# The section ahead of head 0 in 16 slots in place of 20, with projections and maxima moved to earlier slots

## What is computed

```python
qkv = einsum('bte,fe->btf', x, Wqkv); q, k, v = split(...)      # 8 heads, D = 64
q = q + pe;  k = k + pe                                         # positions
scores = where(causal, einsum('bhtd,bhsd->bhts', q, k) / sqrt(D), -inf)
probs = softmax(scores);  attn = einsum('bhts,bhsd->bhtd', probs, v)
x = layernorm(x + einsum('btf,ef->bte', attn, Wo))
x = layernorm(x + ffn(x))                                       # not touched
```

## Time and profile before

| | us |
|---|---|
| Median of 3 runs (732.24 to 735.25) | 733.39 |
| The profiled execution's own time | 734.77 |
| Its span in the trace | 733.0 |
| TensorE busy | 654.5 |
| VectorE / GpSimd / ScalarE busy | 504.9 / 503.1 / 449.2 |
| First score pair of head 0 starts at | 48.29 |

### The profile page before, as it was taken

How to read it: one execution, slowest core, us unless ns; L and a number is a source line. 1 busy time by engine, 2 the same in 40 slices (tenths; PEclk the granted TensorE clock), 3 DMA queues, 4 the chain that set the end, 5 groups by cost and what they waited for, 6 DMA issues and landing times. The chain is left out here.

```text
span 733.0 us, 10119 instructions
## 1 busy us (share of the span) xinstructions
PE 654.5 (89%) x3215; PEld 497.5 (68%) x3215; DVE 504.9 (69%) x1048; ACT 449.2 (61%) x626; POOL 503.1 (69%) x289
## 2 busy tenths in 40 slices
PE   5789999999999999999999999999877899989873
PEld 4557777777777777777677777777667687666651
DVE  3577667667766766866776676674187978877684
ACT  3436666676666666667667666667636577756551
POOL 6016887887878788788787778879943456667560
PEclk9979999999999999999999999999988899999995
DMA  7423211222112221122211232103300000000000
GB/s 186 110 64 70 61 44 45 46 69 60 44 43 49 69 58 44 44 51 69 55 44 44 53 71 51 45 1 91 98 2 1 0 1 1 0 16 0 14 1 29
DMA packets 27460, 33.75 MB, mean 46 GB/s; under 512 B 6897, under 2 KB 13842, under 8 KB 27282
## 3 DMA queue, kind: packets, MB, share of 16 engines
q1 hardware_dynamic: 27410, 33.14, 19.0%
HBM read 6.84 MB, written 1.05 MB: 11 GB/s over the span
## 5 line engine op out<-in xcount | busy, mean ns | idle before, releaser
L313 POOL TENSOR_TENSOR probs_l<-probs,probs_h 128x1024 fp32r<-128x1024 f32 (+1 forms) x160 | 347.5, 2177 | 132.0 <-PE o_ps L536 73.6
L407 DVE TENSOR_REDUCE m_part<-max_ps 128x1 f32<-128x512 f32 (+2 forms) x320 | 181.0, 605 | 111.0 <-PE max_ps L483 79.6
L350 ACT ACTIVATE probs<-scores 128x1024 f32<-128x1024 f32 (+1 forms) x160 | 150.3, 940 | 153.9 <-PE scores L511 96.7
L536 PE MATMUL o_ps<-probs_h,v 128*128 128x512 f32 (+5 forms) x640 | 185.2, 373 | 24.6 <-DVE oh L386 24.1
L353 ACT ACTIVATE probs_h<-scores 128x1024 fp32r<-128x1024 f32 (+1 forms) x160 | 149.8, 936 | 0.0
L536 PEld LDWEIGHTS o_ps<-probs_h,v 128*128 128x128 f32 (+1 forms) x640 | 95.9, 162 | 48.3 <-issue 20.0
L814 POOL TENSOR_TENSOR hid_lo<-hid,hid_hi 128x512 fp32r<-128x512 f32 x64 | 86.6, 1359 | 55.0 <-ACT hid_hi L894 42.3
L510 PE MATMUL scores<-q,k 128*128 128x512 f32 (+1 forms) x320 | 122.8, 384 | 0.0
L511 PE MATMUL scores<-q,k 128*128 128x512 f32 (+1 forms) x320 | 116.9, 365 | 0.0
L536 PE MATMUL o_ps<-probs_l,v 128*128 128x512 f32 (+1 forms) x320 | 116.4, 364 | 0.0
L483 PE MATMUL max_ps<-k,q 128*128 128x512 f32 (+2 forms) x320 | 103.1, 398 | 7.4 <-DVE m_part L407 6.2
(11 more groups left out here) (195 smaller groups left out, 986.9 us busy)
## 6 DMA issues: line engine op xcount, KB each, us to landing
k<-qk SPq DMA_DIRECT2D x96, 128.0 KB, 2.3
q<-qk SPq DMA_DIRECT2D x96, 128.0 KB, 2.3
q<-m_turn SPq DMA_DIRECT2D x128, 0.5 KB
v_all<-L_ffn_ew SPq DMA_DIRECT2D x2, 768.0 KB, 6.5
pos<-positions SPq DMA_DIRECT2D x1, 1024.0 KB, 6.8
out<-v_all SPq DMA_DIRECT2D x4, 256.0 KB, 2.3
acc<-L_attn_Wqkv SPq DMA_DIRECT2D x2, 256.0 KB, 3.9
v_all<-L_attn_Wo SPq DMA_DIRECT2D x2, 256.0 KB, 6.4
```

The costliest lines, as they stand in the source:

```text
L313: pool.tensor_tensor(probs_l[:, p % 2, :, lo:CH], probs[:, p % 2, :, lo:CH], probs_h[:, n % 3, :, lo:CH], ALU.subtract).then_inc(S["probs_ ...
L350: act.activation(probs[:, p % 2, :, lo:CH], scores[:, p % 2, :, lo:CH], ACT.Exp, scale=D ** -0.5).then_inc(S["probs_ready"], 1)
L407: dve.tensor_reduce(m_part[:, r, j:j + 1], max_ps[:, u % 2, 0:width], AX.X, ALU.max).then_inc(S["tile_max_ready"], 1)
L536: last = pe.matmul(o_ps[0:rows, lo:CH], v, pr, start=(p == PAIR0[c] and j == 0 and k == 0), stop=(p == PAIR0[c + 1] - 1 and j == 1 and k = ...
```

## The change

`section(-1)` has NT = 16 slots in place of 20. In it the projections stand at slots 0, 2, 5 and 9 (before 0, 6, 10, 16), each followed by its copies in the slot after (1, 3, 6, 10), and the first 22 pieces of maxima of head 0, two a slot, go from slot 5 to 15 (before 9 to 19). Both are now beside the tiles of v, which stay one a slot in slots 0 to 15. The low half of head 0's v moves from slots 16 and 18 of that section to slots 0 and 1 of `section(0)`. TensorE waits for the copies of all tiles of v ahead of `section(0)`, since the four banks are the scores' from there on. All other sections are as they were.

```diff
+V_HIGH, V_LOW, FIRST_V_LOW = 15, (16, 18), (0, 1)
+FIRST_PROJECT = {0: 0, 2: 1, 5: 2, 9: 3}
+FIRST_UNITS = 5
 def due(table, p, after, h):
+    if h < 0:
+        return [(FIRST_PROJECT[p - after], 0)] if table is PROJECT and p - after in FIRST_PROJECT else []
 def units(p, h):
+    if h < 0:
+        for n in (2 * (p - FIRST_UNITS), 2 * (p - FIRST_UNITS) + 1):
+            if n >= 0:
+                yield 0, n
+        return
             def section(h):
-                for p in range(NP):
+                for p in range(NP if h >= 0 else NT):
@@ VectorE
+            def v_low(h, part):
+                b, ts = h % 2, slice(part * NT // 2, (part + 1) * NT // 2)
+                dve.wait_ge(S["v_high_ready"], h + 1)
+                dve.tensor_tensor(v2[:, b, ts, :], v_all[:, h, ts, :], v1[:, b, ts, 0:D], ALU.subtract).then_inc(S["v_low_ready"], 1)
-                    if p in V_LOW and 0 <= h + 1 < H:
+                    if p in V_LOW and 0 < h + 1 < H:
+                        v_low(h + 1, V_LOW.index(p))
+                    if p in FIRST_V_LOW and h == 0:
+                        v_low(h, FIRST_V_LOW.index(p))
@@ TensorE
             section(-1)
             pe.wait_ge(S["ones_beside_v_made"], 2)
             pe.wait_ge(S["rows_beside_qk_made"], 3)
+            pe.wait_ge(S["v_copied"], NT)
             for h in range(H + 1):
                 section(h)
```

More of the change, by code:

```diff
@@ L115 @@
 OUTPUT = {5: (3, -1), 7: (0, 0), 12: (1, 0), 19: (2, 0)}
-V_HIGH, V_LOW = 15, (16, 18)
+V_HIGH, V_LOW, FIRST_V_LOW = 15, (16, 18), (0, 1)
 DONE = {PAIR0[c + 1] + 2: (c, 0) for c in range(NC)}
+FIRST_PROJECT = {0: 0, 2: 1, 5: 2, 9: 3}
+FIRST_UNITS = 5
 def due(table, p, after, h):
+    if h < 0:
+        return [(FIRST_PROJECT[p - after], 0)] if table is PROJECT and p - after in FIRST_PROJECT else []
     for slot, (c, ahead) in table.items():
```

## The result

| | before | changed |
|---|---|---|
| median of 5 runs, us | 733.13 (732.24 to 735.25) | 740.99 (739.27 to 741.34) |
| profiled execution, us | 734.77 | 741.34 |
| its span, us | 733.0 | 739.5 |

The ratio is 1.0100 with a 95% interval of 1.0077 to 1.0124: 7.9 us slower, where 736.0 and a range of 732.5 to 739.0 were forecast.

What follows compares the result with a forecast made beforehand. The prediction took TensorE, in fixed order, to bound the heads, so only head 0's start could move: +3.55 - 2.15 + 1.25 = +2.65 us on 733.39 gave 736.0 us, range 732.5 to 739.0.

Steps and rivals of the forecast that it cites:

- the two long waits: Ahead of head 0: TensorE idle from about 18.7 to 21.5 us and from 30.4 to 34.4 us.
- the main point: Slot 6: VectorE reduces pieces 2 and 3 only after chunk 2's low part, at 33.77 us; TensorE idles until 34.4.
- First term: Slots ahead of head 0: first score pair at 51.85 us against 48.29, +3.55 us.
- Second term: Head 0's slot 0: first to second score pair takes 2.2 us at the higher clock, before 4.35; -2.15 us.
- Third term: Head 0's low half of v: two pieces, 0.68 us each, delay the first product with v; +1.25 us.
- The second rival: Lower clock persists in slots 11 to 15 or head 0's slot 0: 738.2 to 739.6 us, chance 0.20.
- other place: Sign of failure: the clock at 1.2 GHz in another place than 34 to 39 us.
- The rival that was to be faster: Pieces 2 and 3 reduced near 30.4 us, before the wait for chunk 2: 730.9 or 729.0 us, chance 0.07.
- The prediction's paragraph on ordering: VectorE's queue ahead of head 0: strict FIFO, so waiting reductions cannot pass chunk 2's low part and the sum stands.
- the third rival: Old stalls ahead of head 0 worth as much as new ones: -0.9 to +1.2 us, 732.5 to 734.6, chance 0.23.
- the fourth: Changed kernel faster, with pieces 2 and 3 reduced ahead of chunk 2's wait: 730.9 or 729.0 us, chance 0.07.

Runs made afterwards that it cites:

- e3: Changed kernel with chunk 2's projection at slot 6 in place of 5: 739.40 us, ratio 1.0081.
- e5: The changed kernel run and traced a second time, nothing altered: 740.56 us, ratio 1.0092.
- e2: Changed kernel with both low pieces of head 0's v first in head 0's slot 0: 737.71 us, ratio 1.0059.
- e1: Kernel before with only head 0's two low pieces of v moved, to slots 0 and 1 of head 0: 735.35 us, ratio 1.0028.
- e12: Kernel before with head 0's two low pieces of v moved to the very start of head 0's slot 0: 733.40 us, ratio 0.9997.
- e6: e2 with 15 matmuls that nobody reads added ahead of piece 4: 737.05 us, ratio 1.0048.
- e8: Changed kernel with low v pieces first in head 0, chunk 2 at slot 6, and a later wait for v's last two copies: 736.15 us, ratio 1.0043.
- e10: e8 with unread matmuls in two waits, 11 ahead of chunk 1's projection and 7 ahead of piece 6: 737.05 us, ratio 1.0049.
- e11: Kernel before with chunk 3's projection at slot 13 in place of 16 and unread matmuls ahead of pieces 6 and 12: 734.27 us, ratio 1.0008.
- e7: Kernel before with unread matmuls in two waits, 8 ahead of piece 6 and 9 ahead of piece 18: 730.97 us, ratio 0.9965.
- e9: Kernel before with only the 9 unread matmuls ahead of piece 18: 732.13 us, ratio 0.9989.

## Why the prediction was wrong

**Right.** The prediction was right that TensorE's queue is the kernel's and that a late head 0 shifts the whole: from product 2 (6.31 us late) to the end of the heads (6.23 late) nothing is won back. It was right that chunks 0 to 2 don't move, and on the two long waits: 2.62 and 3.64 us stand where the steps had 2.85 and 4.0. That VectorE's order behind chunk 2's low part is the main point is not borne out: e3 undid it, and the first pair came only 0.5 to 0.9 us earlier.

**First term, +3.55 for the first score pair: 4.33 measured (3.87 in e5).** Nearly all of the difference is chunk 3's high part, 22.12 after the start point where 21.47 was reckoned: its positions were added 0.4 us late (39.98 against 20.52 from the start point), and ScalarE's copy of tile 9, at 40.67, stood ahead of it. From piece 12 (24.18) to the first pair (32.44) took 8.26 us where the steps have 8.25.

**Second term, -2.15 for the clock in head 0's slot 0: -1.92.** 53.91 - 51.48 = 2.43 against 4.35.

**Third term, +1.25 for the low half of v: this is the step that failed.** It took "0.68 each" from the earlier trace rows, a row of a time in which GpSimd does nothing, and used it at a time when GpSimd works. The piece took 2.49. From the second score pair to product 1 the change cost 6.42 - 3.81 = 2.61 us, twice the term; in e2, where no piece is held, it cost 5.13 - 3.81 = 1.32. e1 gives the same move alone, 1.80 us at the first product and 1.9 us of time; e12 gives it without the overlap, 0.

**A low clock in no term.** From product 1 to product 2 took 3.98 us, 2.69 before: another 1.29, at 1.2 GHz. It would be easy to charge this to the held piece too, since TensorE's wait of 2.86 us behind that piece comes just ahead. The runs don't bear that out. In e1 the piece is held and TensorE waits 1.91 us, and no low clock follows; in e2 nothing is held, TensorE waits 1.79 us, and it does. In e6, where the wait of 3.65 us ahead of head 0 is filled, a wait of 1.81 us at the same place is not followed by it. So what TensorE did earlier seems to count as well, and which wait made this stretch stays open. The second rival had a low clock in head 0, but in its first slot and for 2.15 us; by the prediction's own signs, 60 to 63 us is the "other place" that was not to be.

Sum by the trace: 4.33 - 1.92 + 2.61 + 1.29 = 6.31 at product 2, against 2.65. The third term is 1.36 of the 3.66 us between them, the low clock 1.29, the first term 0.78, the second 0.23. With the end of the heads 6.23 late, the start point 1.14 earlier and the rest 1.5 longer this is the 6.5 between the two spans.

**The base.** The medians differ by 7.9, in e5's session by 6.9; the profiled executions by 6.57. The profiled execution of before was 1.6 above its median, that of the changed kernel 0.35. This 0.3 to 1.3 us is in no term. The places of the low clock in setup and rest move single executions by more than that, but that they make this difference is not shown.

**The rival that was to be faster** decided at pieces 2 and 3 ahead of the wait for chunk 2, and e3 has them there, at 28.77. Its first pair came 0.5 to 0.9 us earlier, where 5.1 were reckoned (51.85 to 46.75), and TensorE then waited 2.97 us for chunk 3. The prediction's paragraph on ordering calls it the third rival; it is the fourth.

**What 16 slots cost by themselves.** With low half, chunk 2 and copy wait mended (e8) 2.5 us are left in the medians, 1.35 at the end of the heads. Two waits of the 16 slots stay in its trace: 2.61 us ahead of chunk 1's projection, and 1.8 at piece 26, behind the wait for the high half of v. Filling the first (e10) did not bring it down. That the rest is the order of v's tiles is argued from the steps, not shown.

## What to carry to other kernels

A duration goes with what the other engines do meanwhile: before an instruction is moved, look at what runs beside its new place, and if no row of the trace has it there, bound it by one whole instruction of the engine that may hold it. A VectorE subtraction with both operands in SBUF wants a place where GpSimd is idle; put there, moving it was free. In a stretch where TensorE waits often, a filled wait may be worth more than a better order, but one left open can undo it (e10, e11), and only the median of runs says whether it paid. And before the end of one trace is compared with that of another, look where the clock was low in the parts that nobody changed.

## What the runs showed of the hardware

- A VectorE subtraction of 128 x 512 with two SBUF operands took 0.68 us in all of 16 occurrences before, and 2.49, 2.49, 2.49 and 2.13 us (changed kernel, e5, e3, e1) when it began 0.4 or 0.8 us into a GpSimd subtraction of 2.4 us. Seven of the 16 began inside one too, but only 0.08 us ahead of its end. In e1 it ended 0.56 us after GpSimd's, which is nearly its whole own time: it seems not to run slower but to wait. GpSimd's next instruction, begun inside it, took 1.72 us (changed kernel, e5, e3) and 1.48 (e1) in place of 1.28. Additions that read PSUM and one SBUF operand took 0.67 to 0.70 us beside the same GpSimd work. The Trainium skill (SBUF — State Buffer, section Who interferes with whom) says just this: a VectorE instruction with two SBUF inputs contends with a GpSimd instruction that reads SBUF, and the order of issue decides which of the two is blocked. The traces agree, with the numbers above; the prediction did not weigh it.
- Waits of TensorE of 0.95 to 3.6 us were followed by stretches at 1.2 GHz, not all of them and not at once; of two like waits (1.31 and 1.34 us, e7 and e9) one was followed by none and one by 3.4 us.
- Matmuls that nobody reads held the granted clock at 1.00 from 18 to 69 us in e7 and were worth 2.7 us.
- The start point moves by 2 us between executions (18.38 to 20.51), with the time at which the clock rose in the setup, and the untouched feed-forward part took 203.2 to 207.2 us, with the places of its stretches at 1.2 GHz (e2 against e6: two more of 3.4 us, 3.1 us longer). The span of a single trace is good to some 2 us; the distances within the heads agreed to 0.7 us in the two traces of the changed kernel.
